# Attention in a decoder layer: the transposition of the row maxima four pieces later in TensorE's stream, maxima in two buffers

## What is computed

```python
def self_attn(x, q_heads, k_heads, v_heads, output_proj):      # x: (4, 1024, 512)
    q, k, v = proj(q_heads), proj(k_heads), proj(v_heads)      # (4, 16, 1024, 32)
    scores = einsum('bhqd,bhkd->bhqk', q, k) / sqrt(32)
    scores = where(causal, -inf, scores)
    out = einsum('bhqk,bhkd->bhqd', softmax(scores), v)
    return merge_heads(out) @ output_proj.T

def cross_attn(x, ctx, W_q, W_k, W_v, W_o, b_o):               # ctx: (4, 2048, 512)
    Q, K, V = heads(x @ W_q), heads(ctx @ W_k), heads(ctx @ W_v)
    attn = softmax(einsum('bqhd,bkhd->bhqk', Q, K) / sqrt(32))
    return merge_heads(einsum('bhqk,bkhd->bqhd', attn, V)) @ W_o + b_o
```

## Time and profile before

| | before |
|---|---|
| median of three runs | 4899.39 us |
| profiled execution | 4905.71 us |
| its span | 4904.1 us |
| mean granted clock of TensorE | 0.937 |
| self attention, in the span | about 336 to 1110 us |
| cross attention, in the span | about 1777 to 3720 us |
| TensorE busy | 4388.1 us, 89% |
| VectorE busy | 3038.8 us, 62% |
| GpSimd busy | 2321.7 us, 47% |
| ScalarE busy | 2192.0 us, 45% |

### The profile page before, as it was taken

The page is one execution under the profiler, slowest core; times in us unless marked ns, Lnnn a source line. Parts: engine busy times, 40 slices in busy tenths (PEclk is TensorE's granted clock), DMA queues, the critical chain, the costliest instruction groups (busy, mean ns, idle before and its releaser), DMA issues. The chain is left out here.

```text
span 4904.1 us, 74698 instructions
## 1 busy us (share of the span) xinstructions
PE 4388.1 (89%) x23024; PEld 2724.6 (56%) x23024; DVE 3038.8 (62%) x5530; ACT 2192.0 (45%) x4027; POOL 2321.7 (47%) x790
## 2 busy tenths in 40 slices
PE   7988999997889979999999999999996649898998
PEld 5864555546668854444444444444443427686776
DVE  4436776753633347777777777777772546676776
ACT  1213555551221105666656565556563115544554
POOL 0012333330000017888988888888894123433445
PEclk8987999998889978999999999999998869999999
DMA  4554443406455560222322222222202552322232
GB/s 143 183 164 104 105 106 89 91 16 233 169 178 175 176 159 4 53 58 58 67 53 63 53 63 57 55 53 55 53 6 99 195 181 89 97 95 92 94 108 99
DMA packets 328345, 488.99 MB, mean 100 GB/s; under 512 B 22440, under 2 KB 188328, under 8 KB 321832
## 3 DMA queue, kind: packets, MB, share of 16 engines
q1 hardware_dynamic: 318472, 468.01, 34.3%
q10 hardware_dynamic: 7232, 8.40, 0.6%
q0 software_dynamic: 2304, 8.39, 0.5%
HBM read 315.91 MB, written 168.82 MB: 99 GB/s over the span
## 5 line engine op out<-in xcount | busy, mean ns | idle before, releaser
L851 DVE TENSOR_REDUCE cross_neg_max<-cross_scores 128x1 f32<-128x512 f32 x2048 | 1261.8, 678 | 493.8 <-PE cross_scores L681 493.8
L642 POOL TENSOR_TENSOR cross_partial<-cross_partial,cross_probs 128x2048 f32<-128x2048 f32 x320 | 1464.2, 4576 | 60.6 <-ACT cross_probs L803 35.3
L803 ACT ACTIVATE cross_probs<-cross_shifted 128x512 f32<-128x512 f32 x2048 | 1105.5, 600 | 831.1 <-PE cross_shifted L693 811.0
L681 PE MATMUL cross_scores<-cross_k_stack,cross_q_stack 96*128 96x512 f32 x2048 | 880.4, 442 | 61.7 <-DMA cross_v<-v 32.7
L693 PE MATMUL cross_shifted<-cross_q_stack,cross_k_stack 98*128 98x512 f32 x2048 | 848.9, 421 | 21.3 <-issue 17.6
L693 PEld LDWEIGHTS cross_shifted<-cross_q_stack,cross_k_stack 98*128 98x128 f32 x2048 | 386.5, 190 | 392.6 <-issue 254.6
L681 PEld LDWEIGHTS cross_scores<-cross_k_stack,cross_q_stack 96*128 96x128 f32 x2048 | 397.2, 194 | 328.7 <-DVE cross_neg_max L851 251.0
L803 ACT ACTIVATE self_probs<-self_shifted 128x512 f32<-128x512 f32 (+3 forms) x768 | 359.5, 492 | 385.1 <-PE self_shifted L696 311.1
L851 DVE TENSOR_REDUCE self_neg_max<-self_scores 128x1 f32<-128x512 f32 (+3 forms) x768 | 386.1, 547 | 222.5 <-PE self_scores L684 181.9
L707 PE MATMUL cross_out<-cross_probs,cross_v 128*32 128x512 f32 x4096 | 515.8, 623 | 0.0
L1407 POOL TENSOR_TENSOR experts_v<-experts_u,experts_rows 128x512 f32<-128x512 f32 x128 | 165.2, 1290 | 478.3 <-ACT experts_u L1490 478.3
(11 more groups left out here) (208 smaller groups left out, 6666.7 us busy)
## 6 DMA issues: line engine op xcount, KB each, us to landing
cross_k_stack<-k_hi SPq DMA_DIRECT2D x32, 1024.0 KB, 19.7
experts_yt_hi<-y_hi SPq DMA_DIRECT2D x64, 512.0 KB, 3.9
experts_yt_lo<-y_lo SPq DMA_DIRECT2D x64, 512.0 KB, 4.9
self_q_stack<-q_hi SPq DMA_DIRECT2D x32, 512.0 KB, 7.0
self_k_stack<-k_hi SPq DMA_DIRECT2D x32, 512.0 KB, 14.6
out_a_in<-attn SPq DMA_DIRECT2D x16, 1024.0 KB, 9.7
x<-out_y SPq DMA_DIRECT2D x16, 1024.0 KB, 5.5
kv_x_in<-in_ctx SPq DMA_DIRECT2D x16, 1024.0 KB, 5.8
```

The lines of the kernel that those rows point to most:

```text
L642: nc.gpsimd.tensor_tensor(total, total, own, ALU.add).then_inc(pool_added.sem, 1)
L681: mm = nc.tensor.matmul(scores[at][:, 0:width], q_st[0:96, w, h, q0:q0 + P], k_st[0:96, w, h, half * WIDE:half * WIDE + width], start=True ...
L803: nc.scalar.activation(probs[:, e % NE % PB, h, f:], shifted[n % SHIFTED][:, f:], ACT.Exp).then_inc(exped.sem, 1)
L851: nc.vector.tensor_reduce(neg_max[:, column(a), half:half + 1], scores[n % (SLOTS * ROUNDS) % AHEAD][:, 0:width], AX.X, ALU.max, negate=Tr ...
```

## The change

The transposition no longer is the last slot of its own round, but slot 4 (counted from 0) of the next round: `slot(n)` turns the number of a slot into the round and the piece, with None for the transposition of the round before. The rule in `pieces_at` goes, so that slots are spread by the steps' widths alone. In the cross attention `LEAD` stays 16, and steps 0 to 14 have four slots each and step 15 five; the transposition is the second slot of step 13, behind the shift of head 1. In the self attention `LEAD` grows from 12 to 18; steps 7 to 11 have 6, 5, 4, 3 and 2 slots, and the transposition is the first slot of step 8. `turn_step` is so 13 in the cross attention (it was 12) and 8 in the self attention (as before). The small reduction to `neg` moves out of `turn_rows` to the place behind the last maximum of its round. `neg_max` has two buffers, by the parity of the round. The opening's first slots are the pieces 0 to 3, numbered from 1, and `scored` and `maxed` each get one increment for the slot that isn't there. In the last pass the last transposition is put where the fifth slot would have been, with no piece before it.

```diff
--- before.py
+++ after.py
@@ -408,9 +408,9 @@
                 for half in range(qt // 4 + 1)] if causal else \
                [(h, qt, half, WIDE) for h in range(4) for qt in range(4) for half in range(HALVES)]
     NPIECE = len(parts_of)
-    TURN = NPIECE
+    TURN_AT = 4
     SLOTS = NPIECE + 1
-    LEAD = NPIECE // 4
+    LEAD = 18 if causal else 16
     QTILES = 8 if causal else 4
     COLS = 4 * QTILES
     PB = 4 if causal else 6
@@ -511,12 +511,19 @@
 
     def pieces_at(s):
 
-        def done(m):
-            to = SLOTS * sum(weights[:m]) // sum(weights)
-            before = SLOTS * sum(weights[:max(m - 1, 0)]) // sum(weights)
-            return TURN - LEAD + 1 if before <= TURN - LEAD < to else to
-
+        done = lambda m: SLOTS * sum(weights[:m]) // sum(weights)
         return range(done(s), done(s + 1))
+
+    def slot(n):
+
+        q, at = n // SLOTS, n % SLOTS
+        if at == TURN_AT:
+            return n, q - 1, None
+        return n, q, at - (at > TURN_AT)
+
+    def turn_slot(q, more):
+
+        return (q + 1) * SLOTS + (TURN_AT if more or q + 1 < ROUNDS else 0)
 
     def behind(todo, h):
 
@@ -530,7 +537,7 @@
         v_sb = sb("v", [P, BUFS, SETS, P])
         probs = sb("probs", [P, PB, 4, QB])
         partial = sb("partial", [P, NPARTIAL, 4, QB])
-        neg_max = sb("neg_max", [P, COLS, HALVES])
+        neg_max = sb("neg_max", [P, 2, COLS, HALVES])
         neg = sb("neg", [P, P])
         neg_rows = sb("neg_rows", [P, 2, P], F32R)
         out_sb = sb("out_sb", [P, 2, QB])
@@ -576,9 +583,13 @@
         def stream(r, s, more):
 
             if r == -1:
-                return [n for n in range(SLOTS + LEAD)]
+                opening = [(n + 1, 0, n) for n in range(TURN_AT)]
+                return opening + [slot(n) for n in range(TURN_AT + 1, SLOTS + LEAD)]
             found = [SLOTS * (r + 1) + LEAD + i for i in pieces_at(s)]
-            return [n for n in found if more or n < SLOTS * ROUNDS]
+            if more:
+                return [slot(n) for n in found]
+            last = SLOTS * ROUNDS + TURN_AT
+            return [slot(n) for n in found if n < SLOTS * ROUNDS] + [(SLOTS * ROUNDS, ROUNDS - 1, None)] * (last in found)
 
         def load_heads(sp, bh, w):
             for r, part in ((0, 0), (1, 0), (2, 1)):
@@ -625,7 +636,7 @@
             pool.wait_ge(filled.sem, 1)
             pool.memset(k_st[96:98, :, :, :].bitcast(F32), 1.0).then_inc(filled.sem, 1)
             pool.wait_ge(filled.sem, 2)
-            pool.memset(neg_max[:, :, :], 3.0e38).then_inc(filled.sem, 1)
+            pool.memset(neg_max[:, :, :, :], 3.0e38).then_inc(filled.sem, 1)
             pool.wait_ge(filled.sem, 3)
 
             def add(it, e):
@@ -660,14 +671,15 @@
         @block.tensor
         def _(pe):
             pv_done.give_credit(pe)
+            pe.sem_inc(scored.sem, 1)
             block_done.give_credit(pe)
             sum_done.give_credit(pe)
 
-            def score(it, n):
-                q, a = n // SLOTS, n % SLOTS
+            def score(it, item):
+                n, q, a = item
                 r = q % ROUNDS
                 pe.wait_ge(maxed.sem, maxed.at(it, user_before(n, SLOTS * ROUNDS, AHEAD) + 1))
-                if a == TURN:
+                if a is None:
                     pe.wait_ge(least.sem, least.at(it, q + 1))
                     nc.tensor.transpose(scores[n % (SLOTS * ROUNDS) % AHEAD][:, 0:P], neg[:, :], ident[:, :]).then_inc(scored.sem, 1)
                     return
@@ -803,7 +815,7 @@
                         nc.scalar.activation(probs[:, e % NE % PB, h, f:], shifted[n % SHIFTED][:, f:], ACT.Exp).then_inc(exped.sem, 1)
                         if h == 0 and (more or r + 1 < ROUNDS):
                             if s == turn_step + 1:
-                                write_rows(it, r + 1)
+                                write_rows(it, r + 1, more)
                             if s == turn_step + 2:
                                 load_rows(it, r + 1)
                 if not more:
@@ -820,10 +832,10 @@
                 else:
                     act.wait_ge(sum_done.sem, sum_done.at(it, summed.index(old) + 1 + back * NSUM))
 
-            turn_step = next(s for s in range(NS) if any((LEAD + i) % SLOTS == TURN for i in pieces_at(s)))
-
-            def write_rows(it, q):
-                act.wait_ge(maxed.sem, maxed.at(it, SLOTS * q + SLOTS))
+            turn_step = next(s for s in range(NS) if SLOTS + TURN_AT - LEAD in pieces_at(s))
+
+            def write_rows(it, q, more):
+                act.wait_ge(maxed.sem, maxed.at(it, turn_slot(q, more) + 1))
                 for part in range(2):
                     act.dma_start(neg_dram[part].rearrange("h (t k) -> (h t) k", k=P), neg_rows[0:COLS, part].bitcast(F32)).then_inc(rows_out.sem, 16)
 
@@ -832,35 +844,37 @@
                 q0 = blocks(q % ROUNDS)[0] * QB
                 act.dma_start(q_st[96:98, group(q) % BUFS, :, q0:q0 + COLS * P // 4].bitcast(F32), neg_dram).then_inc(rows_in.sem, 16)
 
-            write_rows(0, 0)
+            write_rows(0, 0, True)
             load_rows(0, 0)
             passes(act, one_pass)
 
         @block.vector
         def _(dve):
             maxed.give_credit(dve)
+            dve.sem_inc(maxed.sem, 1)
             rows_out.give_credit(dve)
 
-            def max_piece(it, n):
-                q, a = n // SLOTS, n % SLOTS
-                if a == TURN:
-                    turn_rows(it, n)
+            def max_piece(it, item):
+                n, q, a = item
+                if a is None:
+                    turn_rows(it, n, q)
                     return
                 _, _, half, width = piece(a)
                 dve.wait_ge(scored.sem, scored.at(it, n + 1))
-                nc.vector.tensor_reduce(neg_max[:, column(a), half:half + 1], scores[n % (SLOTS * ROUNDS) % AHEAD][:, 0:width], AX.X, ALU.max,
+                nc.vector.tensor_reduce(neg_max[:, q % 2, column(a), half:half + 1], scores[n % (SLOTS * ROUNDS) % AHEAD][:, 0:width], AX.X, ALU.max,
                                         negate=True).then_inc(maxed.sem, 1)
-
-            def turn_rows(it, n):
-                q = n // SLOTS
-
-                dve.wait_ge(maxed.sem, maxed.at(it, n))
-                nc.vector.tensor_reduce(neg[:, 0:COLS], neg_max[:, :, :], AX.X, ALU.min).then_inc(least.sem, 1)
+                if a == NPIECE - 1:
+
+                    dve.wait_ge(maxed.sem, maxed.at(it, n + 1))
+                    nc.vector.tensor_reduce(neg[:, 0:COLS], neg_max[:, q % 2], AX.X, ALU.min).then_inc(least.sem, 1)
+
+            def turn_rows(it, n, q):
+                turned = scores[n % (SLOTS * ROUNDS) % AHEAD]
                 dve.wait_ge(scored.sem, scored.at(it, n + 1))
                 dve.wait_ge(rows_out.sem, rows_out.at(it, 2 * q))
-                nc.vector.tensor_copy(neg_rows[0:COLS, 0], scores[n % (SLOTS * ROUNDS) % AHEAD][0:COLS, 0:P]).then_inc(rows_hi.sem, 1)
+                nc.vector.tensor_copy(neg_rows[0:COLS, 0], turned[0:COLS, 0:P]).then_inc(rows_hi.sem, 1)
                 dve.wait_ge(rows_hi.sem, rows_hi.at(it, q + 1))
-                nc.vector.tensor_tensor(neg_rows[0:COLS, 1], scores[n % (SLOTS * ROUNDS) % AHEAD][0:COLS, 0:P], neg_rows[0:COLS, 0].bitcast(F32),
+                nc.vector.tensor_tensor(neg_rows[0:COLS, 1], turned[0:COLS, 0:P], neg_rows[0:COLS, 0].bitcast(F32),
                                         ALU.subtract).then_inc(maxed.sem, 1)
 
             def invert(it, q, part):
```

## The result

| | before | after |
|---|---|---|
| median of four runs each | 4899.02 us | 4826.53 us |
| ratio to before, 95% interval | | 0.985 [0.983, 0.987] |
| profiled execution | 4905.71 us | 4819.18 us |
| its span | 4904.1 us | 4817.6 us |
| mean granted clock of TensorE | 0.937 | 0.944 |

The change takes 72.5 us off the median; 75 were forecast. Of them 72.4 lie between the first and the last reduction into `neg` of the cross attention (1821.6 us before, 1749.2 after) and 4.2 between those of the self attention (668.7 and 664.5). The other 10 lie in stages and openings that the change doesn't touch or hardly touches. A second profile of the same kernel, spans 4826.9 us, has 1753.6 and 664.3 us.

A forecast was written before the change was run, and what follows sets the result against it. TensorE, busy 92 to 94% of both attentions, was taken as held by waits for VectorE, chiefly at the cross attention's transposition. Terms -64 - 16 + 9 - 4 = -75 us gave a median of 4824 us, range 4790 to 4870.

The forecast's parts named there:

- (a): Cross attention, around the transposition: stall and burst go, 2.06 us per round, 64 us over 31 turns (26 to 79).
- R1: Rival, cross attention: only the visible stall goes, the burst's 0.7 us comes back elsewhere, clock unchanged; 4865 us, chance 0.12.
- (b): Cross attention, TensorE's clock behind the turn: ten low stretches of 1.6 us go, 16 us (0 to 16).
- R2: Rival, cross attention: the stall goes but low-clock stretches stay; 4840 us, chance 0.08.
- (c): Cross attention, rows of maxima loaded a step later: first shift waits 0.3 us per round, 9 us more (0 to 19).
- my own sign: Cross attention, first shift of a round: its new wait for the rows stays under 0.6 us; over 1 us means wrong.
- (d): Self attention, steps 7 and 8 around the turn: TensorE held slightly less, -4 us over 15 rounds (-19 to +12).
- (e): Self attention, lead 12 to 18: longer opening against fewer pieces in the rounds, net 0 (-3 to +3 us).
- R3: Rival, cross attention: rows' load much later than read, change loses from 2.7 us lateness per round; 5020 us, chance 0.06.

The follow-up runs named there:

- e1: The kernel before with slots spread over the steps by width alone, the transposition still the last slot of its round: 4961.3 us, ratio 1.012.
- e5: The changed kernel with the cross attention's transposition two pieces behind the last one instead of four: 4836.9 us, ratio 0.986.
- e6: The changed kernel with the cross attention's transposition one piece behind the last, no value block between, and a lead of 18: 4847.2 us, ratio 0.988.
- e3: The changed kernel with the cross attention's load of rows issued behind the third exponential of step 15 instead of the first: 4915.6 us, ratio 1.0025.
- e7: The changed kernel with the self attention's lead at 12 as before instead of 18: 4925.3 us, ratio 1.004.
- e2: The changed kernel with the cross attention's load of rows issued behind the third exponential of step 14: 4824.5 us, ratio 0.986.
- e4: The changed kernel with the skipped score buffer moved to slot 91 of a pass in the cross attention: 4825.2 us, ratio 0.984.

## Why the prediction was right

(a) *Transposition later, cross.* Forecast two stretches of 6.18 us, measured 6.19 (6.27 in some rounds) and 6.09: 2.1 us per round, 65 us over 31 turns (64 forecast). Reading one full stretch as paced by VectorE was right, and so was the split: e1 has the burst taken away and the stall left, and saves 0.77 us per round in the cross attention. R1 (only the stall costs) falls with that. What hides the turn is, it seems, mostly the value block between the last maximum and the transposition: with two pieces and the block nothing is left of the stall (e5), with one piece and no block 0.7 us (e6). The two differ by a piece as well (0.47 us of TensorE's time, where the block has 1.92), so their shares aren't separated. The change's "four pieces" is more than it takes.

(b) *Clock.* Forecast 16 us from ten low stretches gone. All ten are gone. e3 and e7 put the wait at another place and get the low clock there, e6 shortens the stall to 0.7 us and gets none behind the turns. So the link between a stall of this length and the clock is shown, and R2 falls for the turns. Short holds are not always harmless, though: in the last round, which has no pieces, a low stretch came without a longer wait in several of these runs (see the end).

(c) *Rows a step late.* Forecast 0.3 us per round, measured 0.4 on average (0.07 in the first two rounds, up to 0.7 later), 10 us instead of 9; e2 removes it. That the size came out so near is in part luck, for one reading under it was wrong. I took the load's issue, 0.43 us after the first shift of its step, from one early round. It is 0.44 us in the rounds that are written out and 0.67 us in all 24 rounds of the loop (2173.88 to 2174.55), and the kernel before has the smaller value in its written-out rounds and 0.67 us or more in the loop's, so this was to be read before. With 0.67 my own sum gives a wait of 0.4 to 0.8 us. Why the loop's rounds issue it later, and what delays single loads further, wasn't tried. The 2.0 us that I quoted from the Trainium skill (DMA: Bandwidth & Descriptors, "Anatomy of one DMA") stand there for transfers that GpSimd issues; here ScalarE issues the load, and 2.41 to 2.78 us pass from its issue to the first shift, so the wait isn't nil. By my own sign (over 1 us and I am wrong) one wait of 31 failed: the 1.06 us of the last round.

(d), (e) *Self attention.* Forecast -4 us, measured -4.2 over its 15 periods. That is three terms: -3.3 in the rounds, -3.0 in the first period, which holds the opening (forecast 0, -3 to +3), and +2.2 at the long crossing. So the sum is right partly by luck, and the reason was thin. I compared two schedules of VectorE and called the larger lead neutral. It isn't: without it the late rows cost 99 us in this stage (e7). The plain spreading with neither the later transposition nor the larger lead costs 62 (e1).

*What the sum left out.* The skipped score buffer between passes costs 0.6 us in seven rounds, 4 us (e4). And the five long crossings were 8 us cheaper in the first profile after, 4 us in the second: in the first they waited 3.2 us instead of 3.5 and had a shorter low stretch. The crossings vary from kernel to kernel and from profile to profile of one kernel (60.1 to 62.2 us in two profiles of changed). The code says where they are: eight passes, the first and the last written out, make a loop of six, which jumps back five times, and the two short crossings lead into the loop and out of it; the self attention has four passes, one jump back and one long crossing. That TensorE waits there for its instructions is my reading of "issue"; no run shows it, and what sets their length wasn't tried. The terms that I had missed are of opposite signs and small: -65 - 16 + 10 + 4 - 8 = -75 beside the measured -72.4 in the cross attention.

*R3, the rival on the other side.* Its mechanism is real, and closer than I had put it. I set the point from which the change would lose at 2.7 us of lateness per round. In e3 the rows are 1.8 us late and the kernel is slower than before. The failed step is the price: I charged the wait alone, and took the clock's 16 us as fixed, while a wait of this length brings the low clock back and doubles its own cost. With the rows already at the edge of their need by my own sum (0 to 0.6 us late), and 1.4 us more enough to lose, a chance of 0.06 was low.

## What to carry to other kernels

Where an engine that bounds the kernel waits for a result that another has just begun, put the consumer behind work that it has anyway, and look what that moves behind it: here the store and the load of the rows, which went from hidden to 0.4 us late. Read a "busy" stage by the distance between equal milestones (here the value blocks), round by round; that showed the burst, the buffer that was skipped between passes and the late rows, none of which is a large wait in any list. Read such a distance in rounds of the loop and not only in those written out before it: the load's issue differed by 0.24 us between them. Price a new stall of TensorE with the clock that may follow it, and don't take away a rule that looks like a loss in one caller before its other callers have been read.

## What the runs showed of the hardware

How often a low clock (the 1.2 GHz level) followed a wait of TensorE between dense products, by its length:

| idle | where | followed by a low stretch |
|---|---|---|
| 0.6 to 0.8 us | e6, cross, the turn | 0 of 23 |
| 1.3 to 1.4 us | before, cross, the turn | 10 of 31 |
| 1.3 to 1.4 us | e1, cross, the turn | 15 of 31 |
| 1.5 to 2.2 us | e3, cross, the rows | 24 of 26 |
| 2.1 to 2.2 us, and 0.4 us just before | e1, self, the turn | 14 of 14 |
| 1.5 to 2.3 us | e7, self, the rows | 14 of 14 |

A stretch behind 1.4 us cost 1.6 us, so as much again as the stall. Behind 2 us it was often longer, in e7 7 to 14 us of low clock in 13 of 14. What decides in the cases between wasn't tried, and the length of the wait alone doesn't: in last rounds, which have no pieces, 1.06 us (changed) and 0.76 us (e7) were followed by a low stretch. The Trainium skill (TensorE: Matmul & The Clock Gate, "A second HAM failure mode: psum-queue depth-cycling") puts a swinging clock down to frequent micro-idles. Here the holds of 0.3 us for VectorE, 97 of them in the changed kernel's cross attention, brought none. But in the last round of e5, and of e3, e6 and e7, there were low stretches with nothing longer than 0.25 us before them, which agrees with the page. In e5 TensorE had waited 0.2 us for ScalarE in each step or two:

```profile
3624.70 2.54 PE L705 MATMUL cross_shifted<-cross_q_stack,cross_k_stack 98*128 98x512 f32 x5 [0.23 <-ACT cross_probs L815]
3627.17 3.48 PE L719 MATMUL cross_out<-cross_probs,cross_v 128*32 128x512 f32 x16
```
